# Splitting a context into bf16 parts: chunks of 512 columns over eight PSUM banks in place of whole batches over four

## The chip, the cores and the metric

The kernel runs on one core of one Trainium2 chip. The metric is the device time of one execution in microseconds (us); the figure for a version is the median of its runs. "From the span's start" means the time within the one execution that the hardware profiler recorded.

## The reference

The program is a chain of four decoder layers, each with a cross attention and a feed-forward part, on x of 8 batches x 256 tokens x 128 channels, with a context of 8 batches x 1601 rows x 256 channels. The edit concerns only a preparation step of the first cross attention:

```python
# layer 0: 16 heads of 8 channels; keys are the context's first half, then the tokens' own keys
x = x + _L0_xattn_ref(_layernorm(x, axis=-1), ctx_2048, L0_xattn_w_qkv, L0_xattn_w_proj, L0_xattn_b_proj)
...
# layer 1: attention over the context's first half as keys, second half as values, with a mask
x = x + _L1_xattn_ref(ctx_2048, _layernorm(x, axis=-1), mask_BxS2_ik0, L1_xattn_b)
```

Both attentions multiply queries by context keys in float32 precision. The kernel gets this precision from bf16 matmuls: each float32 key is written as a sum of three bf16 numbers, value = p0 + p1 + p2, with p0 = bf16(value), p1 = bf16(value - p0), p2 = bf16(value - p0 - p1). The step computes these three parts of the transposed context keys and stores them in DRAM, where both attentions load them.

## The kernel before

`split_context` (lines 370 to 466) runs once, in the stage `cross0`, as one block: all engines start it together and leave it together. Its input is the first 128 columns of the context, 1601 rows a batch, which lie in `crows`, two buffers of 13 tiles of 128 rows. The first two batches are loaded ahead, during the layer norm. For each of the 8 batches:

- TensorE (L413) transposes the 13 tiles into `psS`, four banks of 512 float32 columns, seen as one flat row of 1601 columns. It waits for the batch's context load and for `rest_done(b)`, the DVE subtraction that last read `psS`.
- ScalarE waits until the store that last read its buffer of `parts` has landed (`stored`, from batch 2 on), waits for the transposes, issues the context load of batch b + 2 (two DMAs, L356 and L357), and copies the flat row to bf16: part 0 (L424).
- VectorE (DVE) subtracts part 0 from the row: `rest` (L452).
- ScalarE copies `rest` to bf16: part 1 (L426).
- VectorE subtracts again: part 2 (L454). In the first six batches it then does one small step of splitting the attention mask (8 rows of 1601: L435, L439, L441, L443, L445, L447).
- SP waits for part 2 and stores the three parts, 1.2 MB (L394).

`parts` and `rest` have two buffers, taken in turn by even and odd batches. SP's order is written out by hand: behind store 3 it waits for the store of the tokens' own parts, for GpSimd's `pool_prepare` (`zeroed`) and for store 0, and issues the first 12 query loads of the attention (`load_queries`, L640); behind stores 4, 5 and 6 it issues 12 key loads each (`load_keys`, L624), which read what the stores 0 to 2 wrote, 8 rows of `key_stack` at a time. At the end SP waits for all stores, and the block closes. GpSimd meanwhile sets the attention's buffers (`pool_prepare`, L664 to L671).

The attention block that follows starts with the keys and queries loaded here.

Of the kernel before, what the change touches and what calls it, by code (L numbers as in the profile page):

```python
# [17 lines left out]
ALU = mybir.AluOpType  # L18
# [3 lines left out]
P = 128  # L22
B, S, D = 8, 256, 128
# [3 lines left out]
KC = 1601  # L27
DC = 256
KB = (KC + P - 1) // P
KTAIL = KC - (KB - 1) * P  # L30
# [4 lines left out]
BANK = 512  # L35
# [316 lines left out]
def load_context(k, sp, dst, b, loaded, columns=slice(0, DC)):  # L352

    src = k.dram["ctx_2048"][:, :, columns]
    whole = (KB - 1) * P
    sp.dma_start(dst[:, 0:KB - 1, :], src[b, 0:whole, :].rearrange("(t p) c -> p t c", p=P)).then_inc(loaded.sem, 16)  # L356
    sp.dma_start(dst[0:KTAIL, KB - 1, :], src[b, whole:KC, :]).then_inc(loaded.sem, 16)  # L357
# [12 lines left out]
def split_context(k, crows, att, own_parts, flags, shift):  # L370


    nc = k.nc
    loaded = [k.flag("ctx_loaded_0"), k.flag("ctx_loaded_1")]
    turned, first, rest_done, second, third = (k.flag(n) for n in ("keys_turned", "split_first", "split_rest", "split_second", "split_third"))
    stored, own_stored = [k.flag("parts_stored_0"), k.flag("parts_stored_1")], k.flag("stored")
    mask_step, mask_stored = k.flag("mask_made"), k.flag("mask_stored")
    flat = k.psS[:].rearrange("p c n -> p (c n)")[:, 0:KC]
    with ExitStack() as mem:  # L379
        rest = k.sb("split_rest", [P, 2, KC], ctx=mem)  # L380
        parts = k.sb("split_parts", [P, 2, 3, KC], BF16, ctx=mem)
        mask, mask_rest = k.sb("mask_rows", [B, KC], ctx=mem), k.sb("mask_rest", [B, KC], ctx=mem)
        mask_parts = k.sb("mask_parts", [B, 3, KC], BF16, ctx=mem)
        block = mem.enter_context(nc.Block())

        @block.gpsimd
        def _(pool):
            att.pool_prepare(pool)

        @block.sync  # L390
        def _(sp):
            for b in range(B):
                sp.wait_ge(*third(b + 1))
                sp.dma_start(k.key_parts[b, :, :, 0:KC].rearrange("j c n -> c j n"), parts[:, b % 2]).then_inc(stored[b % 2].sem, 16)  # L394
                if b == 3:
                    sp.wait_ge(*own_stored(own_parts))
                    sp.wait_ge(*att.zeroed(att.zeroings))
                    sp.wait_ge(*stored[0](16))
                    att.load_queries(sp, 0)
                if b >= 4 and b - 4 < att.RING:  # L400
                    att.load_keys(sp, b - 4)
            for par in range(2):
                sp.wait_ge(*stored[par](16 * (B // 2)))

        @block.tensor
        def _(pe):
            for b in range(B):
                pe.wait_ge(*loaded[b % 2](32 * (b // 2 + 1)))
                if b >= 1:
                    pe.wait_ge(*rest_done(b))  # L410
                for t in range(KB):
                    w = P if t < KB - 1 else KTAIL
                    last = nc.tensor.transpose(k.psS[:, t // 4, (t % 4) * P:(t % 4) * P + w], crows[b % 2][0:w, t, :], k.ident[0:w, 0:w])  # L413
                last.then_inc(turned.sem, 1)

        @block.scalar
        def _(act):
            for b in range(B):
                if b >= 2:
                    act.wait_ge(*stored[b % 2](16 * (b // 2)))  # L420
                act.wait_ge(*turned(b + 1))
                if b + 2 < B:
                    load_context(k, act, crows[b % 2], b + 2, loaded[b % 2], slice(0, D))
                nc.scalar.copy(parts[:, b % 2, 0, :], flat).then_inc(first.sem, 1)  # L424
                act.wait_ge(*rest_done(b + 1))
                nc.scalar.copy(parts[:, b % 2, 1, :], rest[:, b % 2, :]).then_inc(second.sem, 1)  # L426
            act.wait_ge(*mask_step(6))
            act.dma_start(k.mask_parts, mask_parts[:]).then_inc(mask_stored.sem, 16)
            act.wait_ge(*mask_stored(16))

        @block.vector
        def _(dve):
            def split_mask(n):
                if n == 0:
                    last = nc.vector.tensor_scalar(mask[:], flags[:], 1.0, -MASKED, ALU.subtract, ALU.mult)  # L435
                if n >= 1:
                    dve.wait_ge(*mask_step(n))
                if n == 1:
                    last = nc.vector.tensor_scalar(mask[:], mask[:], shift[0:B, 0:1], None, ALU.add)  # L439
                if n == 2:  # L440
                    last = nc.vector.tensor_copy(mask_parts[:, 0, :], mask[:])  # L441
                if n == 3:
                    last = nc.vector.tensor_tensor(mask_rest[:], mask[:], mask_parts[:, 0, :], ALU.subtract)  # L443
                if n == 4:
                    last = nc.vector.tensor_copy(mask_parts[:, 1, :], mask_rest[:])  # L445
                if n == 5:
                    last = nc.vector.tensor_tensor(mask_parts[:, 2, :], mask_rest[:], mask_parts[:, 1, :], ALU.subtract)  # L447
                last.then_inc(mask_step.sem, 1)

            for b in range(B):  # L450
                dve.wait_ge(*first(b + 1))
                nc.vector.tensor_tensor(rest[:, b % 2, :], flat, parts[:, b % 2, 0, :], ALU.subtract).then_inc(rest_done.sem, 1)  # L452
                dve.wait_ge(*second(b + 1))
                nc.vector.tensor_tensor(parts[:, b % 2, 2, :], rest[:, b % 2, :], parts[:, b % 2, 1, :], ALU.subtract).then_inc(third.sem, 1)  # L454
                if b < 6:
                    split_mask(b)
    for par in range(2):
        loaded[par].passed(32 * (B // 2))
        stored[par].passed(16 * (B // 2))
    for sig in (turned, first, rest_done, second, third):  # L460
        sig.passed(B)
    own_stored.passed(own_parts)
    mask_step.passed(6)
    mask_stored.passed(16)
# [436 lines left out]
def cross0(k):  # L901
# [9 lines left out]
    with ExitStack() as mem:  # L911
# [44 lines left out]
        own_done.passed(1)  # L956
        own_copied.passed(1)
        split_context(k, crows, att, own_parts, flags, shift)
        split.close()
        out = k.sb("att_out", [P, QT, B * D], ctx=mem)  # L960
# [2634 lines left out]
```

## Time and profile before

| | us |
|---|---|
| median of 3 runs | 4140.33 |
| runs, lowest to highest | 4135.44 to 4140.78 |
| profiled execution, own time | 4139.14 |
| its span | 4137.1 |
| start of L413's first transposes in the span | 67.5 |
| first DMA of the next block | 147.35 |

Over the span TensorE's matmuls are busy for 3676.2 us (89%), VectorE 2683.1 (65%), ScalarE 2281.6 (55%), GpSimd 1350.8 (33%). In the stretch from 67 to 147.4 us it is otherwise: TensorE 23.1 us, VectorE 44.6, ScalarE 24.2, GpSimd 32.6 of 80.4 us, at a mean granted TensorE clock of 0.53 and a DMA share of 0.64. A row of the timeline gives start and duration in us, engine, line, operation, what is written and read, and in square brackets how long the engine sat idle before it and what ended that. A line ending in q (ACTq, SPq) is an engine's own DMA issue.

### The profile page before, as it was taken

The numbers are of one execution on the slowest core, as the hardware profiler recorded it, in microseconds if no ns is written. First come the engines' busy times: TensorE is split into PE (matmuls) and PEld (weight loads), VectorE is DVE, ScalarE is ACT, GpSimd is POOL, SyncE is SP. The second block draws the span as 40 slices with busy tenths as digits, with TensorE's granted clock in tenths as the row PEclk, the third lists the DMA queues.
The fourth block names the chain that finished last, engine by engine and source line by source line (L and its number), as shares of the span: only waits on it lengthen the run. The fifth ranks groups of instructions, "written<-read, shape, count | busy, mean of one in ns | idle before, by whom it ended". The sixth has DMA issues, their size and how long they took to land. (4 is left out here: it accounts for less than half of the span.)

```text
span 4137.1 us, 72514 instructions
## 1 busy us (share of the span) xinstructions
PE 3676.2 (89%) x28012; PEld 2206.1 (53%) x28017; DVE 2683.1 (65%) x4526; ACT 2281.6 (55%) x3856; POOL 1350.8 (33%) x1655
## 2 busy tenths in 40 slices
PE   3699999889699985997799999999999999999654
PEld 2233333478444434674456666666666666666441
DVE  4799999544577736554356666666656666666647
ACT  2599999633377752222156566666656566656330
POOL 3011111220011104220045565555555556556310
PEclk7699999999799987998899999999999999999877
DMA  4332231002165401000100000000000000000010
GB/s 140 128 62 50 50 63 42 20 18 46 48 94 82 58 2 31 2 2 10 49 16 17 1 17 1 1 17 1 17 1 17 1 17 1 1 1 1 7 37 20
DMA packets 117718, 122.91 MB, mean 30 GB/s; under 512 B 19008, under 2 KB 95648, under 8 KB 116992
## 3 DMA queue, kind: packets, MB, share of 16 engines
q1 hardware_dynamic: 104184, 111.20, 12.2%
q10 hardware_dynamic: 13200, 7.16, 0.6%
q8 instruction: 221, 3.62, 0.4%
q14 instruction: 113, 0.93, 0.1%
HBM read 102.51 MB, written 15.68 MB: 29 GB/s over the span
## 5 line engine op out<-in xcount | busy, mean ns | idle before, releaser
L2101 DVE TENSOR_TENSOR att_highest.1<-att_highest.1,psS 128x1024 f32<-128x1024 f32 (+1 forms) x320 | 356.6, 1114 | 369.2 <-ACT prob_0.1 L2035 181.8
L869 DVE TENSOR_REDUCE att_peak.1<-psS 128x1 f32<-128x512 f32 (+1 forms) x1024 | 579.2, 633 | 19.8 <-PE psS L744 13.4
L839 ACT ACTIVATE att_probT.1<-psT 128x512 f32<-128x512 f32 (+1 forms) x682 | 366.6, 568 | 29.2 <-PE psT L773 9.9
L2192 POOL TENSOR_TENSOR key_sums_0.1<-key_sums_0.1,prob_0.1 128x512 f32<-128x512 f32 x256 | 326.5, 1275 | 28.7 <-POOL key_sums_0.1 L2192 0.4
L2192 POOL TENSOR_TENSOR key_sums_1.1<-key_sums_1.1,prob_1.1 128x512 f32<-128x512 f32 x256 | 325.8, 1273 | 28.7 <-POOL key_sums_1.1 L2187 0.4
L869 DVE TENSOR_REDUCE att_peak.2<-psS 128x1 f32<-128x512 f32 (+1 forms) x512 | 261.6, 568 | 78.7 <-PE psS L744 75.8
L790 PE MATMUL psM<-att_probT.1,quad_values.1 128*9 128x256 f32 (+1 forms) x3840 | 291.9, 382 | 0.2 <-issue 0.2
L744 PE MATMUL psS<-key_stack.1,query_stack.1 64*128 64x512 bf16 (+1 forms) x1024 | 253.6, 379 | 25.2 <-PEq L379 16.2
L2122 DVE TENSOR_TENSOR prob_0.1<-prob_0.1,psO 128x1024 f32<-128x1024 f32 (+1 forms) x256 | 244.0, 1016 | 49.0 <-PE psO L1951 49.0
L2122 DVE TENSOR_TENSOR prob_1.1<-prob_1.1,psO 128x1024 f32<-128x1024 f32 (+1 forms) x256 | 243.9, 1016 | 49.0 <-PE psO L1951 49.0
L2187 POOL TENSOR_TENSOR key_sums_0.1<-prob_0.1 128x512 f32<-128x512 f32 x64 | 82.0, 1282 | 576.1 <-ACT prob_0.1 L2041 576.1
L2035 ACT COPY prob_0.1<-psS 128x1024 f32<-128x1024 f32 (+1 forms) x224 | 203.8, 954 | 72.6 <-PE psS L1930 72.1
L2035 ACT COPY prob_1.1<-psS 128x1024 f32<-128x1024 f32 (+1 forms) x224 | 203.7, 954 | 71.8 <-PE psS L1930 71.4
L773 PE MATMUL psT<-query_stack.1,key_stack.1 64*128 64x256 bf16 x1279 | 212.9, 275 | 9.6 <-ACT att_probT.1 L839 9.5
L1897 PE MATMUL psM<-ctxT_0.1,wkv.1 128*128 128x512 f32 (+1 forms) x512 | 215.5, 544 | 2.7 <-ACT keyT_0.1 L2018 1.4
L1930 PE MATMUL psS<-qT_1.1,keyT_1.1 64*128 64x256 f32 x1664 | 214.5, 392 | 2.0 <-DVE att_highest.1 L2101 2.0
L1930 PE MATMUL psS<-qT_0.1,keyT_0.1 64*128 64x256 f32 x1664 | 214.5, 392 | 1.0 <-ACT keyT_0.1 L2018 0.7
L1907 PE MATMUL psT<-wkv.1,ctxT_1.1 128*128 128x128 f32 (+1 forms) x1664 | 214.7, 280 | 0.1
L1907 PE MATMUL psT<-wkv.1,ctxT_0.1 128*128 128x128 f32 (+1 forms) x1664 | 214.4, 280 | 0.0
L1907 PEld LDWEIGHTS psT<-wkv.1,ctxT_1.1 128*128 128x128 f32 (+1 forms) x1664 | 192.1, 187 | 37.5 <-issue 36.9
L1907 PEld LDWEIGHTS psT<-wkv.1,ctxT_0.1 128*128 128x128 f32 (+1 forms) x1664 | 192.1, 187 | 37.2 <-issue 36.1
L1897 PE MATMUL psM<-ctxT_1.1,wkv.1 128*128 128x512 f32 (+1 forms) x512 | 211.5, 536 | 0.0
(688 smaller groups left out, 7511.4 us busy)
## 6 DMA issues: line engine op xcount, KB each, us to landing
key_stack.1<-key_parts SPq DMA_DIRECT2D x384, 58.0 KB
key_stack.2<-key_parts SPq DMA_DIRECT2D x96, 200.1 KB
ctx_rows.1<-in_ctx_dram SPq DMA_DIRECT2D x8, 1536.0 KB
key_parts<-split_parts.2 SPq DMA_DIRECT2D x8, 1200.8 KB, 7.5
ctx_keys_0.1<-in_ctx_dram ACTq DMA_DIRECT2D x4, 768.0 KB
ctx_keys_1.1<-in_ctx_dram ACTq DMA_DIRECT2D x4, 768.0 KB
query_stack.1<-query_parts SPq DMA_DIRECT2D x192, 16.0 KB
ctx_values_0.1<-in_ctx_dram SPq DMA_DIRECT2D x4, 768.0 KB
```

What stands on the lines that cost most here:

```text
L744: self.k.nc.tensor.matmul(self.score_bank[m % 3][:, 0:w], self.queries(rows, g, h, s * P, P), self.keys(rows, g, h, c0, w), start=True, st ...
L773: last = self.k.nc.tensor.matmul(self.key_bank[(m + h) % 3][0:w, n * S:(n + 1) * S], self.keys(rows, g, h, col, w), self.queries(rows, g, ...
L790: last = self.k.nc.tensor.matmul(self.partial[32 * j:32 * j + self.hd + 1, :], self.vquad[0:w, q % 2, blk, j, :], self.probT[0:w, g % self ...
L839: self.k.nc.scalar.activation(probs[:, blks[0]:blks[-1] + 1, :].rearrange("p b q -> p (b q)"), bank[0:w, 0:len(blks) * S], ACT.Exp).then_i ...
L869: self.k.nc.vector.tensor_reduce(self.peak[:, 2 * h + s, c:c + 1], self.score_bank[m % 3][:, 0:w], AX_X, ALU.max).then_inc(self.peak_done. ...
L1897: last = nc.tensor.matmul(bank[:, 0:w], self.wkv[:, t, p * P:(p + 1) * P], self.ctxT[b % 2][:, t, n * BANK:n * BANK + w], start=(t == 0), ...
L1907: last = nc.tensor.matmul(bank[0:w, kb % 4 * P:(kb % 4 + 1) * P], self.ctxT[b % 2][:, t, kb * P:kb * P + w], self.wkv[:, t, at:at + P], st ...
L1930: last = nc.tensor.matmul(k.psS[:, 2 * (g % 2) + h, blk % 2 * S:(blk % 2 + 1) * S], self.keyT[i % 2][own, blk * P:(blk + 1) * P], self.qT[ ...
L2035: nc.scalar.copy(self.prob[i % 2][:, :, at:at + w], k.psS[:, 2 * (g % 2):2 * (g % 2) + 2, 0:w]).then_inc(self.kept.sem, 1)
L2101: self.k.nc.vector.tensor_tensor(own, old, new, ALU.max).then_inc(self.raised.sem, 1)
L2122: self.k.nc.vector.tensor_tensor(own, own, by, ALU.add).then_inc(self.lowered.sem, 1)
L2192: nc.gpsimd.tensor_tensor(acc, acc, own[:, h, c * BANK:(c + 1) * BANK], ALU.add).then_inc(self.summed.sem, 1)
```

## The change

The unit of work becomes a chunk of at most 512 columns, that is four tiles; a batch has `CH` = 4 chunks, three of 512 and one of 65 columns, and the chunks are numbered m = 0 to 31 through all batches. Chunk m goes to bank m mod 8: the four banks of `psS`, two of `psT`, `psM` and `psO`. TensorE waits for the subtraction of chunk m - 8. ScalarE and VectorE do each of their two passes a chunk at a time, and each issues the second pass of chunk m - 1 behind the first pass of chunk m. All semaphores count chunks. ScalarE issues the context load of batch b + 2 behind the first copy of the batch's last chunk, and no longer ahead of the first copy of the batch. The mask step of a batch stands behind the second pass of its third chunk.

```diff
-    flat = k.psS[:].rearrange("p c n -> p (c n)")[:, 0:KC]
+    banks = [k.psS[:, n, :] for n in range(4)] + [k.psT[:, 0, :], k.psT[:, 1, :], k.psM[:], k.psO[:].rearrange("p a n -> p (a n)")]
+    CH = (KC + BANK - 1) // BANK
...
-                sp.wait_ge(*third(b + 1))
+                sp.wait_ge(*third(CH * (b + 1)))
...
                 pe.wait_ge(*loaded[b % 2](32 * (b // 2 + 1)))
-                if b >= 1:
-                    pe.wait_ge(*rest_done(b))
-                for t in range(KB):
-                    w = P if t < KB - 1 else KTAIL
-                    last = nc.tensor.transpose(k.psS[:, t // 4, (t % 4) * P:(t % 4) * P + w], crows[b % 2][0:w, t, :], k.ident[0:w, 0:w])
-                last.then_inc(turned.sem, 1)
+                for m in range(CH * b, CH * (b + 1)):
+                    if m >= len(banks):
+                        pe.wait_ge(*rest_done(m - len(banks) + 1))
+                    for t in range(m % CH * 4, min(m % CH * 4 + 4, KB)):
+                        w = P if t < KB - 1 else KTAIL
+                        last = nc.tensor.transpose(banks[m % len(banks)][:, t % 4 * P:t % 4 * P + w], crows[b % 2][0:w, t, :], k.ident[0:w, 0:w])
+                    last.then_inc(turned.sem, 1)
...
+            def second_part(m):
+                par = m // CH % 2
+                act.wait_ge(*rest_done(m + 1))
+                nc.scalar.copy(parts[:, par, 1, columns(m)], rest[:, par, columns(m)]).then_inc(second.sem, 1)
+
+            for m in range(CH * B):
+                b, par = m // CH, m // CH % 2
+                if m % CH == 0 and b >= 2:
+                    act.wait_ge(*stored[par](16 * (b // 2)))
+                act.wait_ge(*turned(m + 1))
+                nc.scalar.copy(parts[:, par, 0, columns(m)], banks[m % len(banks)][:, 0:width(m)]).then_inc(first.sem, 1)
+                if m % CH == CH - 1 and b + 2 < B:
+                    load_context(k, act, crows[par], b + 2, loaded[par], slice(0, D))
+                if m >= 1:
+                    second_part(m - 1)
+            second_part(CH * B - 1)
...
+            def third_part(m):
+                par = m // CH % 2
+                dve.wait_ge(*second(m + 1))
+                nc.vector.tensor_tensor(parts[:, par, 2, columns(m)], rest[:, par, columns(m)], parts[:, par, 1, columns(m)],
+                                        ALU.subtract).then_inc(third.sem, 1)
+
+            for m in range(CH * B):
+                par = m // CH % 2
+                dve.wait_ge(*first(m + 1))
+                nc.vector.tensor_tensor(rest[:, par, columns(m)], banks[m % len(banks)][:, 0:width(m)], parts[:, par, 0, columns(m)],
+                                        ALU.subtract).then_inc(rest_done.sem, 1)
+                if m >= 1:
+                    third_part(m - 1)
+                if m % CH == CH - 1 and m // CH < 6:
+                    split_mask(m // CH)
+            third_part(CH * B - 1)
```

The old loops of ScalarE and VectorE go; the load, store and SP order are otherwise as before.

## Rows read from the trace of the kernel before

**Rows 1.** Waits from 67 to 147 us: who waited for whom, total, times, longest

```profile
PE psS L413 <- DVE split_rest.1 L452: 33.5, 6, 7.2
...
ACT split_parts.2 L424 <- DMA key_parts<-split_parts.2: 7.1, 2, 5.5
```

**Rows 2.** Timeline of one batch from 110 to 119 us, and the last transposes

```profile
110.62 2.90 PE L413 MATMUL psS<-tables.1,ctx_keys_1.1 128*128 128x128 f32 x13 [4.82 <-DVE split_rest.1 L452]
...
113.61 0.38 ACTq L356 DMA_DIRECT2D ctx_keys_1.1<-in_ctx_dram  x1
...
114.84 1.49 ACT L424 CAST split_parts.2<-psS 128x1601 bf16<-128x1601 f32 x1 [2.81 <-issue]
116.37 1.82 DVE L452 TENSOR_TENSOR split_rest.1<-psS,split_parts.2 128x1601 f32<-128x1601 f32 x1 [1.59 <-ACT split_parts.2 L424]
...
118.34 2.90 PE L413 MATMUL psS<-tables.1,ctx_keys_0.1 128*128 128x128 f32 x13 [4.82 <-DVE split_rest.1 L452]
...
128.45 2.93 PE L413 MATMUL psS<-tables.1,ctx_keys_1.1 128*128 128x128 f32 x13 [7.20 <-DMA ctx_keys_1.1<-in_ctx_dram]
```

**Rows 3.** Groups by form, whole span: busy us, mean ns, then idle before

```profile
L424 ACT CAST split_parts.2<-psS 128x1601 bf16<-128x1601 f32 x8 | 12.0, 1495 | 44.1 <-issue 37.0 <-DMA key_parts<-split_parts.2 7.1
...
L2018 ACT COPY keyT_0.1<-psM 128x512 f32<-128x512 f32 x96 | 56.3, 586 | 101.1 <-PE psM L1897 101.1
...
L2018 ACT COPY keyT_0.1<-psM 128x65 f32<-128x65 f32 x32 | 6.9, 214 | 2.6 <-PE psM L1900 2.6
...
L452 DVE TENSOR_TENSOR split_rest.1<-psS,split_parts.2 128x1601 f32<-128x1601 f32 x8 | 14.6, 1820 | 14.6 <-ACT split_parts.2 L424 14.6
...
L884 DVE TENSOR_TENSOR att_out.1<-psO,att_rtotal.1 128x64 f32<-128x64 f32 x32 | 7.2, 225 | 1.1
...
L1016 DVE TENSOR_TENSOR X.1<-psS,X.1 128x512 f32<-128x512 f32 x4 | 2.8, 692 | 1.2 <-PE psS L999 1.2
```

**Rows 4.** Timeline of POOL's memsets and three mask steps of DVE

```profile
80.63 19.55 POOL L671 MEMSET key_stack.1<- 3x11142 bf16 x2
...
85.89 4.97 DVE L439 TENSOR_SCALAR mask_rows.1<-mask_rows.1,logit_shift.1 8x1601 f32<-8x1601 f32 x1
...
95.94 5.08 DVE L441 CAST mask_parts.1<-mask_rows.1 8x1601 bf16<-8x1601 f32 x1
...
113.81 0.97 DVE L445 CAST mask_parts.1<-mask_rest.1 8x1601 bf16<-8x1601 f32 x1
```

**Rows 5.** Timeline of SP's DMA issues, from 100 to 148 us

```profile
106.68 6.83 SPq L640 DMA_DIRECT2D query_stack.1<-query_parts  x12
...
114.34 6.68 SPq L624 DMA_DIRECT2D key_stack.1<-key_parts  x12
121.64 0.38 SPq L394 DMA_DIRECT2D key_parts<-split_parts.2  x1
...
128.95 4.55 SPq L624 DMA_DIRECT2D key_stack.1<-key_parts  x12
138.93 0.38 SPq L394 DMA_DIRECT2D key_parts<-split_parts.2  x1
147.35 0.40 SPq L356 DMA_DIRECT2D ctx_values_0.1<-in_ctx_dram  x1
```

**Rows 6.** Landings: the eight stores of L394; then store 5 alone (121.5 to 122)

```profile
DMA to landing us min/median/max: 5.9/7.5/11.8
...
key_parts<-split_parts.2 SPq DMA_DIRECT2D x1, 1200.8 KB, 10.5
```

**Rows 7.** Queue packets, MB, share: 110 to 112 (two rows), 121 to 127, 135 to 138

```profile
q1 hardware_dynamic: 219, 0.70, 86.9%
q10 hardware_dynamic: 214, 0.11, 18.1%
...
q10 hardware_dynamic: 274, 0.13, 12.2%
...
q1 hardware_dynamic: 190, 0.58, 50.9%
```

More of the change, by code:

```diff
@@ L377, in split_context, with columns, width @@
     mask_step, mask_stored = k.flag("mask_made"), k.flag("mask_stored")
-    flat = k.psS[:].rearrange("p c n -> p (c n)")[:, 0:KC]
+    banks = [k.psS[:, n, :] for n in range(4)] + [k.psT[:, 0, :], k.psT[:, 1, :], k.psM[:], k.psO[:].rearrange("p a n -> p (a n)")]
+    CH = (KC + BANK - 1) // BANK
+    def columns(m):
+        return slice(m % CH * BANK, min(m % CH * BANK + BANK, KC))
+    def width(m):
+        return min(BANK, KC - m % CH * BANK)
     with ExitStack() as mem:
@@ L408, in _ @@
                 pe.wait_ge(*loaded[b % 2](32 * (b // 2 + 1)))
-                if b >= 1:
-                    pe.wait_ge(*rest_done(b))
-                for t in range(KB):
-                    w = P if t < KB - 1 else KTAIL
-                    last = nc.tensor.transpose(k.psS[:, t // 4, (t % 4) * P:(t % 4) * P + w], crows[b % 2][0:w, t, :], k.ident[0:w, 0:w])
-                last.then_inc(turned.sem, 1)
+                for m in range(CH * b, CH * (b + 1)):
[5 more added lines that the diff above has]
+                    last.then_inc(turned.sem, 1)
         @block.scalar
         def _(act):
[L418 to L426, printed above, removed]
+            def second_part(m):
[13 more added lines that the diff above has]
+            second_part(CH * B - 1)
             act.wait_ge(*mask_step(6))
@@ L448, in split_mask @@
                 last.then_inc(mask_step.sem, 1)
[L450 to L456, printed above, removed]
+            def third_part(m):
[13 more added lines that the diff above has]
+            third_part(CH * B - 1)
     for par in range(2):
@@ L460, in split_context @@
     for sig in (turned, first, rest_done, second, third):
-        sig.passed(B)
+        sig.passed(CH * B)
     own_stored.passed(own_parts)
```

## The prediction

> **What bounds the kernel now.** I first asked which piece of the kernel the edit touches. The timeline shows `split_context` as one closed stretch: its first transposes start at 67.5 us, and the next block begins when SP has seen the last store land, at about 147 us (its first DMA is at 147.35) [rows 5]. Nothing outside this stretch of 80 us is edited, and both ends are barriers, so the question is only where the 147 moves.
>
> Inside, the waits come next [rows 1]. TensorE's 33.5 us are waits for the DVE subtraction of the batch before: the one set of four banks. Two more waits are for transfers: ACT's 7.1 us for stores, and TensorE's 7.2 us for context load 7, at 128.45 [rows 2]. No engine is full; the stretch is a chain. Its undisturbed link, read from the timeline [rows 2]: transposes 2.90, two DMA issues and gaps 1.3, ACT copy 1.5, DVE 1.8, and the next transposes start 7.7 us after the last ones.
>
> But three things cut across that chain. First, the mask steps: L439 and L441 last 5.0 and 5.1 us, while L445, of the same size and type, lasts 0.97 [rows 4]. The two slow ones end at 90.86 and 101.02, just behind the two POOL memsets of L671, which together run from 80.63 to 100.18. I read this as DVE waiting for the POOL instruction to end. Second, SP: behind store 3 it issues 12 query loads (6.8 us) and behind stores 4, 5 and 6 twelve key loads each (6.7 us, the last 4.55) [rows 5]; a store stands behind them in SP's order. Third, the transfers: stores land 5.9 to 11.8 us after their issue [rows 6], and the late ones share engines with key loads and context loads [rows 7].
>
> **What the edit takes away.** With eight banks, the transposes of batch b+1 no longer wait for the subtractions of batch b. The serial 7.7 us become, for a batch, the sum of the busiest engine. DVE: (3 x 0.692 + 0.225) x 2 = 4.6 us, with eight gaps of 0.03 to 0.04 us 4.9 [rows 3]; before it was 2 x 1.82. ACT: (3 x 0.586 + 0.214) x 2 = 3.9 us, gaps 0.3, and two DMA issues 1.2, so 5.4. So chunking adds about 1.3 us of DVE work a batch but would save 2 to 3 us of the period, some 15 to 20 us over the stretch, if nothing else bound it.
>
> **What it adds: a tie that isn't in the sketch.** DVE does the first subtraction of chunk m before the third part of chunk m-1. So the last third part of batch b (chunk 4b+3), which releases store b, comes behind the first subtraction of batch b+1. That needs ACT's first copy of b+1, and this copy waits for (1) store b-1, landed, and (2) all of context load b+1, transposed. So two stores never overlap: store b is issued after store b-1 landed, plus 0.586 + 0.692 + 0.225 and gaps, 1.6 us. Before, store b needed only its own batch. With a landing of 5.9 us (the least [rows 6]; before, load and store were issued within a us of each other, 113.61 and just ahead of 114.34, and now the load comes about 3 us behind the store) the step is 7.5 us, near the old 7.7; with 7.5 it is 9.1.
>
> The Trainium skill, "DMA: Bandwidth & Descriptors" (Anatomy of one DMA), fits a DMA's time as 2.0 us plus bytes over 436e3 per us, for the GpSimd path. For a store's 1.23 MB that estimate is 4.8 us, and the step 6.4. The least row here is 5.9, so the trace is slower than the page, and the sum keeps 5.9.
>
> **The sum, in us from the span's start.** The mask steps are moved too: they stand in front of the last third part of their batch. DVE starts at about 69 and has two batches (5.5 each, with what ACT's DMA issues hold it up) and L435 with a wait (3) behind it when it reaches L439: 83. That is inside the first memset of L671 (80.6 to about 90), so it leaves with its end, at 91.4 (90.86, and 0.5 by which I let the earlier L435 push POOL, an estimate). It reaches L441 at about 97, in the second memset, and leaves at 101.6. So the early saving is swallowed, and store 2 goes at 101.6 + 0.692 + 0.225 and gaps = 102.6. From there:
> - Store 3: 102.6 + 7.5 = 110.1. SP then issues queries until 110.1 + 0.5 + 6.8 = 117.4.
> - Store 4: the later of 117.4 and 110.1 + 7.5, 117.6. Key loads 0 issue until 124.7.
> - Store 5: the later of 124.7 and 117.6 + 7.5, 125.1 (before 121.6).
> - Context load 7 is now issued behind ACT's last first copy of batch 5: batch 5 starts at 116.0 and gets there about 3.7 us later, 119.7, against 113.6 before [rows 2].
> - It lands late. Before it took until 128.4, 14.8 us [rows 2]. It can only use what the other queue leaves: with a store both queues pass about equal packets (219 to 214 in 2 us), and while the keys pass it moves only 274 packets in 6 us [rows 7]. The key loads alone keep the share at 51%, so about half of the engines carry them; on that half load 7 has some 800 of its 1,601 packets. It now starts together with key loads 0 (from 121.7, 6 us, some 280 packets), then runs beside store 5 (3.5 us, 192), then key loads 1 (4 to 6 us, 200 to 280), and the small rest is quick. That is 121.7 + 6 + 3.5 + 5 and a lag of 1.3: 137.5. By the old 14.8 us it would be 134.5; the ends I keep are 133 and 141.
> - Store 6: 137.5 + 0.95 for four transposes + 1.6 = 140.05 (before, by the key loads behind it at 128.95, about 128.5).
> - Key loads 2: 0.4 + 4.55, to 145.0. Batch 7 ends computing at 137.5 + 0.95 + 0.6 + 4.9 + 0.3 = 144.3, so SP decides: store 7 at 145.0 (before 138.93). Before, the next block's first DMA came 8.4 us behind it [rows 5]; with that it comes at 153.4.
>
> Against 147.35 the difference is +6.1 us. The last landing is unsure by some -2 to +2.5 us (5.9 for the least, 10.5 for store 5, which also was issued right behind key loads). The profiled execution took 4139.14 us (span 4137.1 and 2.0 around it); with +6 that is 4145.1. The median of the runs is 1.2 higher, so I predict 4146.
>
> What lies beside other work: the added ACT and DVE work after batch 2 (about 5.3 us a batch lie inside the step of 7.5; without that cover they'd cost 1.3 a batch, 6.5 in all). TensorE's 104 transposes are the same. The mask steps behind batches 3 to 5 (1.8, 1.0, 1.8) still fit in the step. PSUM banks used anew have no other user in the stretch.
>
> **Rivals.**
> - *Landings stay as they were (slower).* If stores 2 to 4 land in 7.5 us and store 5 in 10.5, the steps are 9.1: store 3 at 111.7, store 4 at 120.8, load 7 lands at about 141, store 6 at about 143.5, store 7 at 148.5, the next block with 10.5 + 0.4 at 159.4: +12 us, 4152. For it: the median landing before was 7.5. Against: the context load issued beside most of them is gone from there. It decides when the mean landing is above 6.7 us, or load 7 lands after 139.7.
> - *Load 7 isn't late.* If it gets its packets through by 132.6, when store 5 has landed (125.1 + 7.5), then store 6 goes at 134.2, store 7 at 139.2, the next block 147.6 to 150.1: +0.3 to +2.8, so 4141 to 4143. For it: the half of the engines that carries no keys is free. Against: the load needs both halves, and the other is never free from 121.7 on.
> - *The edit does what it says (faster).* If DVE's pace of 5.3 us set the batches behind 101.6, SP would be next: store 3 at 108, queries to 115, keys to 122, 127 and 132, store 7 at 132, the next block 138.3 to 142.9: -4.4 to -9, so 4131 to 4136. It needs store b to be free of store b-1; I see no way in the order of the waits.
> - *The edit changes nothing measurable* is then mostly the first forecast: 0.2% is 8.3 us, about what a measurement of this kernel can tell from no change.
>
> **Chances.** Load 7 late, between 133 and 141: 0.60 (of this 0.13 above +8.3). Old landings: 0.18, of which 0.16 above. Load not late: 0.14, all within. Faster rival: 0.08, of which 0.04 below -8.3. Sum: faster 0.04, same 0.67, slower 0.29. The forecast's own range is 4141.5 to 4150; for 8 in 10 I add the two milder rivals and half of the slow one: 4138 to 4152.
>
> **What the changed profile would show.** TensorE without waits for L452's successor in batches 0 and 1, and the first eight chunks transposed in one run by 74 us. Two mask steps still ending near 91 and 101.5. Store issues about 7.5 us apart between store 2 and store 5, each 1.6 us behind the landing before. ACT's longest waits for stores at batches 4 to 6. TensorE waiting for load 7 until about 137.5. SP's last store directly behind key loads, near 145. The prediction fails if DVE isn't held at the two memsets, if stores land in well over 6 us, or if load 7 lands outside 133 to 141.

## The result and the profile after

The changed kernel takes 4147.62 us, the median of 22 runs, against 4141.0 us for the kernel before, also of 22 runs; the ratio is 1.0015, with a 95% interval of 1.0008 to 1.0021. By that ratio it is 6.2 us slower (3.3 to 8.7), next to the forecast of +6; the medians are 6.6 us apart. The interval leaves out zero, and lies for the most part within the 8.3 us (0.2%) below which the forecast spoke of "nothing measurable". The profiled execution of the changed kernel was a long one, with a span of 4149.4 us, 12.3 us above that of the profile before; so I read from it only the edited block. Its ends are GpSimd's first memset (all engines enter together) and the next block's first matmul. Before, these stood at 67.53 and 147.54: 80.0 us. Now they stand at 66.67 and 155.48: 88.8 us. The block starts 0.9 us earlier for reasons outside it, and is 8.8 us longer: 2.6 us more than the times say. Each block length here comes from one profile, and over all kernels below it agrees with the times within some 3 us.

Lines have moved: the transposes are L422, the first copy L437, the second L430, the subtractions L475 and L469, the store L402, the query loads L665, the key loads L649, the context load still L356 and L357.

The waits from 66 to 156 us, as in [rows 1]:

```profile
PE psT L422 <- DMA ctx_keys_1.1<-in_ctx_dram: 31.3, 3, 17.3
...
PE psS L422 <- DMA ctx_keys_0.1<-in_ctx_dram: 21.0, 3, 10.5
...
ACT split_parts.2 L437 <- PE psT L422: 12.3, 1, 12.3
```

TensorE's waits for the subtraction are gone, all 33.5 us of them. In their place stand 52.3 us of waits for context loads: six loads, one of 17.3 us. TensorE was relieved of one wait and stands in the next.

SP's issues, as in [rows 5]. From the first row, stores 0 to 3 (by narrower stretches of the same view they go at 77.65, 90.98, 101.16 and 108.45):

```profile
77.65 31.16 SPq L402 DMA_DIRECT2D key_parts<-split_parts.2  x4
108.94 6.15 SPq L665 DMA_DIRECT2D query_stack.1<-query_parts  x12
115.94 0.38 SPq L402 DMA_DIRECT2D key_parts<-split_parts.2  x1
116.36 6.09 SPq L649 DMA_DIRECT2D key_stack.1<-key_parts  x12
124.68 0.38 SPq L402 DMA_DIRECT2D key_parts<-split_parts.2  x1
125.11 4.28 SPq L649 DMA_DIRECT2D key_stack.1<-key_parts  x12
140.89 0.38 SPq L402 DMA_DIRECT2D key_parts<-split_parts.2  x1
141.31 7.24 SPq L649 DMA_DIRECT2D key_stack.1<-key_parts  x12
148.60 0.38 SPq L402 DMA_DIRECT2D key_parts<-split_parts.2  x1
155.29 0.40 SPq L356 DMA_DIRECT2D ctx_values_0.1<-in_ctx_dram  x1
```

The gap to look at is from 124.68 to 140.89: 16 us between stores 5 and 6, where 7 were before. What fills it shows in the timeline of the other engines around 139 us:

```profile
138.21 1.97 PE L422 MATMUL psT<-tables.1,ctx_keys_1.1 128*128 128x128 f32 x8 [17.27 <-DMA ctx_keys_1.1<-in_ctx_dram]
139.41 0.59 ACT L437 CAST split_parts.2<-psT 128x512 bf16<-128x512 f32 x1 [12.26 <-PE psT L422]
...
140.04 0.69 DVE L475 TENSOR_TENSOR split_rest.1<-psT,split_parts.2 128x512 f32<-128x512 f32 x1 [12.15 <-ACT split_parts.2 L437]
...
140.64 0.22 DVE L469 TENSOR_TENSOR split_parts.2<-split_rest.1,split_parts.2 128x65 bf16<-128x65 f32 x1
```

Read it downwards: context load 7 lands, TensorE transposes, ACT copies the first chunk of batch 7, DVE subtracts it, and only then comes the small row at 140.64, the third part of batch 6's last chunk. All of batch 6 had been ready since 127.9 but for its last chunk of 65 columns: ACT's second copy (0.25 us, at 139.90, also held behind batch 7's first copy) and these 0.22 us. Store 6 follows at 140.89. This is the tie of the forecast.

DVE's mask steps and POOL's memsets, as in [rows 4]:

```profile
73.06 3.83 DVE L451 TENSOR_SCALAR mask_rows.1<-mask_flag_rows.1 8x1601 f32<-8x1601 int32 x1
...
82.39 7.84 DVE L455 TENSOR_SCALAR mask_rows.1<-mask_rows.1,logit_shift.1 8x1601 f32<-8x1601 f32 x1
...
95.74 4.66 DVE L457 CAST mask_parts.1<-mask_rows.1 8x1601 bf16<-8x1601 f32 x1
```

```profile
66.67 9.38 POOL L689 MEMSET key_stack.1<- 128x11142 bf16 x1 [66.23 <-POOLq L968]
...
80.01 19.55 POOL L696 MEMSET key_stack.1<- 3x11142 bf16 x2
```

The second step was reached 3.5 us earlier than before (82.39 for 85.89) and lasted 2.9 us longer (7.84 for 4.97). It ends at 90.23, where it ended at 90.86 before: its end hangs on the memset, not on its start. So all that the chunks gained in batches 0 and 1 was lost there.

The prices of a chunk were close to those taken from [rows 3]: 678 to 690 ns for DVE's steps where the sum has 692, 584 ns for ACT's first copy where it has 586, and 621 ns for the second copy, which had no row of its own. Groups by form of the stretch:

```profile
L430 ACT CAST split_parts.2<-split_rest.1 128x512 bf16<-128x512 f32 x24 | 14.9, 621 | 26.8 <-DVE split_rest.1 L475 23.4 <-issue 3.3
L475 DVE TENSOR_TENSOR split_rest.1<-psS,split_parts.2 128x512 f32<-128x512 f32 x12 | 8.1, 678 | 2.2 <-ACT split_parts.2 L437 2.2
L437 ACT CAST split_parts.2<-psS 128x512 bf16<-128x512 f32 x12 | 7.0, 584 | 22.2 <-PE psS L422 17.9 <-DMA key_parts<-split_parts.2 4.3
```

The landings of the eight stores, as in [rows 6]; then store 5 alone:

```profile
DMA to landing us min/median/max: 5.6/5.9/10.7
...
key_parts<-split_parts.2 SPq DMA_DIRECT2D x1, 1200.8 KB, 10.7
```

### The profile page after: what moved, and what is told of

It reads as the page before. It is cut to its first block and busy times, and to the rows that moved or that the text cites. A ratio compares the mean times of both kernels' runs of the same rounds, so it can differ in the third digit from the quotient of the medians.

```text
span 4149.4 us, 72609 instructions
## 1 busy us (share of the span) xinstructions
PE 3681.3 (89%) x28012; PEld 2210.1 (53%) x28017; DVE 2691.0 (65%) x4574; ACT 2287.4 (55%) x3904; POOL 1353.9 (33%) x1655
## 5 line engine op out<-in xcount | busy, mean ns | idle before, releaser
L894 DVE TENSOR_REDUCE att_peak.2<-psS 128x1 f32<-128x512 f32 (+1 forms) x512 | 261.7, 568 | 78.9 <-PE psS L769 76.0
```

The source lines that it names most:

```text
L894: self.k.nc.vector.tensor_reduce(self.peak[:, 2 * h + s, c:c + 1], self.score_bank[m % 3][:, 0:w], AX_X, ALU.max).then_inc(self.peak_done. ...
```

## The experiments

Ten kernels ran beside the two above. The block's length is from the profile, between the two ends named above; the ratio is that of the times to the kernel before. The two last columns are for load 7, the context load of batch 7, and key loads 0, the first set of 12 key loads: ACT's issue of it and the first issue of key loads 0, and when TensorE, waiting for it, went on (its landing, where it did wait).

| kernel | block, us | against before | ratio (95%) | load 7 issued / key loads 0 | load 7 landed |
|---|---|---|---|---|---|
| before | 80.0 | | | 113.6 / 114.3 | 128.5 |
| changed | 88.8 | +8.8 | 1.0015 (1.0008 to 1.0021) | 116.6 / 116.4 | 138.2 |
| untie | 78.0 | -2.0 | 0.9996 (0.9987 to 1.0005) | 111.8 / 110.9 | 131.1 |
| keys_last | 83.4 | +3.4 | 1.0006 (0.9997 to 1.0015) | 114.9 / 131.7 | 122.8 |
| mask_late | 78.2 | -1.8 | 1.0003 (0.9994 to 1.0012) | 108.2 / 108.0 | 125.6 |
| four_banks | 87.1 | +7.1 | 1.0019 (1.0010 to 1.0028) | 116.9 / 116.8 | 137.0 |
| early_load | 78.9 | -1.1 | 0.9997 (0.9988 to 1.0006) | 109.1 / 114.6 | 116.2 |
| before_mask | 76.6 | -3.4 | 0.9991 (0.9982 to 1.0001) | 108.4 / 108.9 | not waited for |
| untie_mask | 72.1 | -8.0 | 0.9973 (0.9962 to 0.9985) | 107.9 / 104.4 | 123.2 |
| all | 69.6 | -10.4 | 0.9975 (0.9965 to 0.9985) | 103.1 / 104.3 | 108.9 |
| all_four | 71.9 | -8.1 | 0.9975 (0.9965 to 0.9984) | 103.1 / 103.7 | 117.9 |
| all_keys | 69.4 | -10.6 | 0.9969 (0.9959 to 0.9980) | 104.4 / 112.4 | 110.1 |

**untie: the last parts of a batch inside the batch.**

```diff
-                if m >= 1:
-                    second_part(m - 1)
-            second_part(CH * B - 1)
+                if m % CH >= 1:
+                    second_part(m - 1)
+                if m % CH == CH - 1:
+                    second_part(m)
```

and the same for `third_part` on VectorE, ahead of the mask step.

> The changed kernel with the last second and third part of a batch done within the batch, so that store b no longer stands behind the first subtraction of batch b+1 (and with it behind the landing of store b-1 and behind context load b+1). If this tie costs the time: stores 1 and 2 go at about 83 and 96 us instead of 91 and 101, store 3 at 106, stores 5 and 6 at 121 to 129, the last store at 138 to 142 instead of 148.6; the time falls by 7 to 10 us from the changed kernel, to within 3 us of the kernel before. If the added instructions and shorter copies are the cost (rival), the stores stay where they are within 1 us and the time stays 6 us above the kernel before.

SP's issues in that run:

```profile
104.32 6.06 SPq L667 DMA_DIRECT2D query_stack.1<-query_parts  x12
110.43 0.38 SPq L402 DMA_DIRECT2D key_parts<-split_parts.2  x1
...
117.04 0.38 SPq L402 DMA_DIRECT2D key_parts<-split_parts.2  x1
...
122.02 0.38 SPq L402 DMA_DIRECT2D key_parts<-split_parts.2  x1
122.45 5.96 SPq L651 DMA_DIRECT2D key_stack.1<-key_parts  x12
137.12 0.38 SPq L402 DMA_DIRECT2D key_parts<-split_parts.2  x1
```

Store 6 goes at 122.02, 18.9 us earlier, although load 7 still lands late (131.06). The last store stands at 137.12. The block is 10.8 us shorter than the changed kernel's, with the same chunks and eight banks. So the tie is what turned the late load into a late end; the number of instructions isn't the cost. (Stores 1, 2 and 3 went at 80.3, 93.7 and 103.8, some 2 to 3 us earlier than I had put them, and store 5 at 117.04, where I had put it at 121 or later.)

**keys_last: SP's key loads behind the last store.**

```diff
-                if b >= 4 and b - 4 < att.RING:
-                    att.load_keys(sp, b - 4)
+            for q in range(att.RING):
+                att.load_keys(sp, q)
             for par in range(2):
                 sp.wait_ge(*stored[par](16 * (B // 2)))
```

> The changed kernel with SP's three sets of key loads issued behind the last store instead of behind stores 4, 5 and 6. If context load 7 is late because the key loads share half of the engines with it: TensorE's wait for it (17.3 us, until 138.2) shrinks to under 8, load 7 lands by 124, store 6 goes at about 131 and store 7 at about 137; the key loads then add some 15 us behind it, so the next block starts at 151 to 154 and the time is 1 to 4 us below the changed kernel. If load 7 is late for another reason (its own descriptors, the stores), it still lands after 132 and the time grows by 5 us or more.

```profile
122.79 1.97 PE L422 MATMUL psT<-tables.1,ctx_keys_1.1 128*128 128x128 f32 x8 [3.48 <-DMA ctx_keys_1.1<-in_ctx_dram]
```

```profile
114.26 17.42 SPq L402 DMA_DIRECT2D key_parts<-split_parts.2  x4
131.72 15.83 SPq L649 DMA_DIRECT2D key_stack.1<-key_parts  x36
```

The tie is still in, but load 7 lands 7.9 us after its issue and no longer 21.7; the wait for it is 3.5 us and no longer 17.3. Only the key loads were moved. The last store is issued at 131.3, 17.3 us earlier, and the 36 issues of the key loads (15.8 us) take most of that back: the next matmul is at 148.4, where I had put the next block at 151 to 154. Stores 6 and 7 go at 128.0 and 131.3 and not at 131 and 137; stores 5 and 6 landed in 4.5 us each, quicker than any of the changed kernel's. The time, 3.3 us below the changed kernel's by the medians, is as expected.

**mask_late: two mask steps each behind batches 3, 4 and 5.**

```diff
-                if m % CH == CH - 1 and m // CH < 6:
-                    split_mask(m // CH)
+                if m % CH == CH - 1 and 3 <= m // CH < 6:
+                    split_mask(2 * (m // CH) - 6)
+                    split_mask(2 * (m // CH) - 5)
```

> The changed kernel with the six mask steps of VectorE moved behind batches 3, 4 and 5, two each, when GpSimd's memsets are over. If the steps that wait for a memset swallow the early saving: they take 1.0 to 1.8 us each, store 1 goes at about 85 and store 2 at 93 (91.0 and 101.2 before), store 3 at about 100, the first query load at about 100 (held by GpSimd's end) and the next block starts 6 to 9 us earlier: about the time of the kernel before, within 3 us. If the late context load alone sets the end and the early stall is harmless (rival), the block ends within 2 us of the changed kernel's.

```profile
91.65 5.77 DVE L451 TENSOR_SCALAR mask_rows.1<-mask_flag_rows.1 8x1601 f32<-8x1601 int32 x1
97.45 1.04 DVE L455 TENSOR_SCALAR mask_rows.1<-mask_rows.1,logit_shift.1 8x1601 f32<-8x1601 f32 x1
...
104.03 0.98 DVE L457 CAST mask_parts.1<-mask_rows.1 8x1601 bf16<-8x1601 f32 x1
```

The two steps that lasted 7.8 and 4.7 us last 1.04 and 0.98 now that no memset runs; the first one, reached a bit too early, waits in their place until 97.42, 0.85 us behind the end of POOL's memsets (77.78 + 18.79 = 96.57 in that run). The early batches run on (stores 1, 2 and 3 at 79.7, 86.9 and 99.25), the block is 10.6 us shorter, more than the 6 to 9 expected; the time is that of the kernel before, as expected. The rival, that the early stall is harmless, is out.

**four_banks: only the four banks of `psS` in the list.**

> The changed kernel with chunks going round four banks instead of eight, nothing else. If, as I hold, no wait of TensorE for a bank is on the path that sets the end: the time stays within 2 us of the changed kernel's (about 6 us above the kernel before), and TensorE waits for banks only in batch 1. If the eight banks earn time that the tie hides, it is 4 us or more slower than the changed kernel.

87.1 us, 1.7 us shorter than the changed kernel in this profile, and 1.0019 in time: no difference that the runs can tell. As the change stood, four of its eight banks earned nothing that the runs show. Not as expected: TensorE waited for the subtraction in four batches, not one; none of these waits reached the end.

**early_load: the context load back at the start of the batch.**

This is not quite the order of before: there the load stood ahead of the batch's first copy, but behind ACT's wait for the store (`stored`); here it stands ahead of that wait too.

```diff
                 b, par = m // CH, m // CH % 2
+                if m % CH == 0 and b + 2 < B:
+                    act.wait_ge(*turned(m + CH))
+                    load_context(k, act, crows[par], b + 2, loaded[par], slice(0, D))
                 if m % CH == 0 and b >= 2:
...
-                if m % CH == CH - 1 and b + 2 < B:
-                    load_context(k, act, crows[par], b + 2, loaded[par], slice(0, D))
```

> The changed kernel with one thing undone: the context load of batch b+2 is issued ahead of the batch's first copy (and of the wait for a store), as it was before the change. Load 7 is then issued at about 113 us instead of 116.6, ahead of store 4 and key loads 0. If its lateness comes of starting together with the key loads, it lands by about 131 instead of 138.2, and then store 5's landing (124.7 + 10.7 = 135.4) is next: store 6 at about 137 instead of 140.9, and the time is 3 to 5 us below the changed kernel (0.3 to 3 us above the kernel before). If the queue's order doesn't matter (rival), it lands within 2 us of 138 and nothing changes.

```profile
116.17 1.97 PE L422 MATMUL psT<-tables.1,ctx_keys_1.1 128*128 128x128 f32 x8 [4.75 <-DMA ctx_keys_1.1<-in_ctx_dram]
```

```profile
128.82 0.59 ACT L440 CAST split_parts.2<-psT 128x512 bf16<-128x512 f32 x1 [4.67 <-DMA key_parts<-split_parts.2]
```

Right in sign, too small in size. Load 7 is issued at 109.1 (I had put 113), 5.5 us ahead of the key loads, and lands 7.1 us later, at 116.2 (I had put 131). Batch 7 then waits for store 5, at 128.82, as expected, but that one lands in 7.1 us and no longer in 10.7. It has the same key loads behind it, but no context load beside it; that this is the reason is likely, not shown by itself. The block is 9.9 us shorter than the changed kernel's, where I had reckoned with 3 to 5; the time is within noise of the kernel before.

**before_mask: the kernel before with the mask steps behind batches 3 to 5, as in mask_late.**

> The kernel before with its six mask steps moved behind batches 3, 4 and 5, two each, when GpSimd's memsets are over; no chunks. If the two slow steps wait for GpSimd's memsets: they take 1.0 us each, stores 2 and 3 go at about 94 and 101 instead of 96.0 and 106.2, the last store at about 134 instead of 138.9 and the time falls by 3 to 6 us (ratio 0.9985 to 0.9993). If they are slow for themselves or the path is set by the transfers of the end (rival), no change.

The two steps take 1.04 and 0.98 us here too; the block is 3.4 us shorter, the ratio 0.9991. The interval reaches 1.0001, so the times alone don't prove that the kernel gets faster; block length and steps agree with it.

**untie_mask: both edits together.**

> The changed kernel with both repairs of the first set: the last parts of a batch done within the batch, and the mask steps behind batches 3 to 5. The two causes should add, since one sets the stores up to 101 us and the other those behind: store 3 waits in SP's order no more than for GpSimd's end at 99, stores 4, 5, 6 at about 106, 113 and 119, load 7 is issued by 106 and lands by 123, the last store at about 129.5, and the time is 8 to 12 us below the kernel before (0.9971 to 0.9981). If both repaired the same us (rival), it is at most 3 us below.

72.1 us, and 0.9973: 0.27% or 11 us below the kernel before by the ratio, 8.4 by the medians, 8.0 by the block. Alone each of the two gave 10.6 to 10.8 us against the changed kernel, together 16.8, not the 21.4 of causes that add. Load 7 is late here as well (13.8 us of wait, until 123.2), as its issue still falls beside the key loads.

**all: and the context load early.**

> As the run before it (untied, mask steps late), and the context load of batch b+2 issued at the start of batch b. Load 7 is then no longer the last thing to arrive; what is left is SP's order (queries and key loads behind GpSimd's end at 99) and the landing of store 5. Time 0 to 3 us below the run before it, 8 to 14 us below the kernel before. The rival: the earlier loads run into the stores, and it gains nothing or loses up to 2 us.

69.6 us and 0.9975. Load 7 lands 5.8 us after its issue. The block is another 2.4 us shorter, which the times can't tell from untie_mask. The rival came true in part: the context loads now run beside the stores, and stores 0 to 3 land in 7.8 to 8.4 us, where untie_mask has 5.5 to 7.0.

**all_four and all_keys: the best version with four banks, and with the key loads one store later.**

> The best version so far (untied, mask steps late, context loads early) with chunks going round four banks instead of eight. If the banks are worth little once the other waits are gone, since a chunk's bank is free as soon as VectorE has read it and four transposes take 0.9 us: the block is at most 2 us longer than that version's 69.6 us, the time still 8 to 11 us below the kernel before. If the eight banks carry the gain (rival), the context loads, which can only be issued when all four chunks of a batch are transposed, slip and it gives back 5 us or more.

> The same version with each set of key loads one store later (behind stores 5, 6 and 7). If SP's order and the keys' half of the engines set its end: stores 5 and 6 go at about 110 and 116 and land in under 9 us, the last store at about 122, the last key loads are issued by 127 and the next block starts 2 to 4 us earlier. If the total of the transfers is the limit (rival), the end stays within 1.5 us.

Four banks cost 2.3 us of the block, and nothing that the times show (0.9975 both). Load 7 is issued at the same 103.1 but lands 14.8 us later and no longer 5.8; store 4 follows it by 0.2 us there, and by 0.8 in all. The packets of the queues (q10 is ACT's, with the load; q1 is SP's, with the store) from 106.1 to 108.1 us show what tips it, first in all, then in all_four:

```profile
q10 hardware_dynamic: 1031, 0.52, 88.9%
q1 hardware_dynamic: 37, 0.12, 14.7%
```

```profile
q1 hardware_dynamic: 209, 0.67, 82.9%
q10 hardware_dynamic: 276, 0.14, 23.3%
```

In all the load is nearly through before the store's packets come. In all_four the two pass about packet for packet, the store's being six times as large, and what is left of the load then meets the key loads. The 2.3 us come with this shift of 0.5 us between two issues, so they aren't a clean price of four banks.

Moving the key loads gives 0.2 us, within the 1.5 of the rival. Its reason isn't borne out, though: the total of the transfers is no limit at the end, where the DMA share is 0.51 from 128 to 134 us. Stores land in 8.4 us in the middle and up to 13.1. The end of the block in all_keys:

```profile
123.64 0.38 SPq L402 DMA_DIRECT2D key_parts<-split_parts.2  x1
124.06 5.07 SPq L653 DMA_DIRECT2D key_stack.1<-key_parts  x12
137.17 0.40 SPq L356 DMA_DIRECT2D ctx_values_0.1<-in_ctx_dram  x1
```

The last store is issued 25 us earlier than in the changed kernel, but takes 13 to land, with key loads in front and behind. With the share at half, I read the end as set by the half of the engines that carries the key loads; no run isolates it.

## Why the prediction was right

The mechanism was right: the order of the waits, what stands behind what, and what ends last. Not every size was, and load 7's landing came out so close by luck, as told below. Step by step, forecast and profile after (which starts 0.9 us earlier):

| step | forecast | measured |
|---|---|---|
| DVE leaves the two held mask steps | 91.4, 101.6 | 90.2, 100.4 |
| store 2 | 102.6 | 101.2 |
| store 3 | 110.1 | 108.5 |
| store 4 | 117.6 | 115.9 |
| store 5 | 125.1 | 124.7 |
| load 7 issued, landed | 119.7, 137.5 | 116.6, 138.2 |
| store 6 | 140.05 | 140.9 |
| store 7 | 145.0 | 148.6 |
| next block's first DMA | 153.4 | 155.3 |

- **The tie** held, as put. Stores 3 and 4 go 1.6 and 1.5 us behind the landing before them (101.16 + 5.7 = 106.9, then 108.45; 108.45 + 6.0 = 114.4, then 115.94). untie takes it away and the block falls by 10.8 us.
- **The held mask steps** held, and mask_late showed their cause from the other side: 1.0 us when no memset runs.
- **Landings of 5.9 us** was the right bound to take: 5.6 to 6.0 for stores 0 to 3. Over all eight the mean is 6.5 us, under the 6.7 that the rival with old landings needed. Two stores were slower: store 4 took 6.6 us, and store 5 took 10.7, as that rival had it; that cost nothing, since load 7 landed still later (138.2 against 124.7 + 10.7 = 135.4).
- **The late context load** was right in its landing and cause (keys_last and early_load), but two of its terms were off and cancelled. It was issued 3.1 us earlier than I had it: batch 5 started at 114.5 and not at 116.0, and from there ACT took 2.1 us and not 3.7, since I reckoned with DVE's pace where ACT copies the first parts in a bunch behind each wait. And it took 21.7 us to land, not 17.8. That the two cancel is luck. The packets didn't come as I had shared them out either. The load's queue moved these from 121.7 to 127.7, from 128 to 134, and from 134 to 138:

```profile
q10 hardware_dynamic: 963, 0.49, 49.0%
...
q10 hardware_dynamic: 290, 0.14, 10.4%
...
q10 hardware_dynamic: 44, 0.02, 2.1%
```

 So at 128 only some 330 packets were left, where my sharing leaves about 520 (800 less 280), but these 330 took until 138. From 134 to 138 the other queue's share stands at 50.7% beside the load's 2.1. That fits half of the engines being idle while the load's rest waits on the other half, as I had it; no view shows the halves apart.
- **The reading of the half** in [rows 7] was wrong, though its figure was right. The 50.9% from 135 to 138 are not the key loads alone: store 6 was under way from 128.53 until 140.3. The clean figure is that of keys_last from 140 to 146 us, behind the last landing (131.3 + 6.2 = 137.5), with nothing but key loads:

```profile
q1 hardware_dynamic: 372, 0.92, 51.6%
```

- **Key loads 2** is the term that was mis-sized: 7.24 us of issue where I took 4.55. With store 6 0.85 us late, that put store 7 at 148.6 instead of 145.0. In [rows 5] they were issued as quickly as 4.55; over the profiles here the set took 4.55 to 7.72 (4.55 in untie_mask, 4.66 in all, 5.96 in untie, 7.35 in early_load, 7.72 in before_mask); what decides it is open. The last landing gave 1.7 us back (6.2 + 0.5 in place of 8.4), so the next block came 1.9 us later than forecast, and 2.8 with the earlier start of the block. The times came out at +6.2 for a forecast of +6; as the block grew by 8.8 us, this match is closer than the sum was.
- **The Trainium skill's fit** ("DMA: Bandwidth & Descriptors", Anatomy of one DMA), which is for the GpSimd path, gave an estimate of 4.8 us for a store. The trace of the changed kernel doesn't reach it: 5.6 us at the least and 5.9 in the median, over stores that SP issues. Landings of 4.5 us occur in untie and keys_last.
- **The faster rival** could not come, as the forecast said, while the order of the waits stood. With the order alone mended (untie) the block is 2.0 us shorter than before; it took the late mask steps as well (untie_mask, 8.0 us) to get what that rival promised, 4.4 to 9.

One thing the forecast didn't see: the three causes don't add. Any one of untie, mask_late or early_load takes away 9.9 to 10.8 us of block, more than the whole loss of 8.8. In these runs the end is latest when load 7 starts beside key loads 0 and store 6 hangs on load 7, and the early stall decides how late both start. The forecast's sum has this chain, but I then took its causes for separate ones: the expectation of untie_mask says that they should add.

## What to carry to other kernels

When a loop is skewed by one ("second pass of m-1 behind first pass of m"), look at what the last piece of a group releases: here 65 columns of a finished batch stood behind the next batch's load and the store before, and the double buffer was gone. A wait in a hand-written order costs by what stands behind it in the queue, not by its own length. And before giving a stage more banks, ask which wait comes second: here the banks' 33.5 us turned into 52 us of waits for loads, and even in the mended version the extra four banks were worth at most 2.3 us of a block of 72, in one profile each, and nothing in the times.

## What the runs showed of the hardware

- **Loads that fill half of the DMA share hold back others.** Key loads (12 a set, 0.7 MB, 8 rows each) keep the DMA share at about half when they run alone: 51.6% in keys_last. A context load of 0.8 MB issued beside them took 14.8 to 21.7 us to land in seven kernels (before, changed, untie, mask_late, four_banks, untie_mask, all_four); in the four others where TensorE waited for it, 5.7 to 7.9 us (all, all_keys, early_load, keys_last), and three of these issue it over 5 us away from the first key load. The fourth, all, issues it 1.2 us ahead of it. With keys_last, where only the key loads were moved, the hold is shown; that it is by sharing half of the engines is read from the share.
- **A DMA issue gets longer behind another queue's.** The second of ACT's two context DMAs took 0.7 to 0.8 us in untie when the store came after it, and 2.4 us in the changed kernel when SP had issued a store some 0.6 us ahead; 3.86 us with key loads as well. Values between (1.3 us in the changed kernel's first batch, 1.7 in early_load) occur with no store just ahead. From the changed kernel, and then from untie, where the load precedes the store:

```profile
109.48 2.47 ACTq L357 DMA_DIRECT2D ctx_keys_0.1<-in_ctx_dram  x1
...
116.96 3.86 ACTq L357 DMA_DIRECT2D ctx_keys_1.1<-in_ctx_dram  x1
```

```profile
101.37 0.74 ACTq L357 DMA_DIRECT2D ctx_keys_1.1<-in_ctx_dram  x1
```

 ACT's copies stand behind it in order, so DVE idles 1.6 us ahead of L469 in batches 1 to 4 (3.0 in batch 5). No run isolates what in the issue waits.
- **DVE and GpSimd's memsets.** One-input steps of DVE in SBUF (8x1601) were held to the end of a running memset in every profile in which they met one, for up to 9.5 us; the two-input subtractions at the same times weren't (0.69 us each, as always). The held steps end 0.85 us behind the memset (76.05 and 76.89 in the changed kernel). The Trainium skill, "SBUF — State Buffer" (SBUF: two separate sides), has this as a port pair that the first comer holds for its whole instruction. It names DVE operations in a two-port mode as contenders, and those with two SBUF inputs only against a GpSimd operation that reads SBUF, which a memset doesn't. The profiles agree as to who is held and how long; no view names the mode.
